# Layer 0's rounded exponential: written by ScalarE, or copied by GpSimd

## The chip, the cores and the metric

The kernel runs on one core of a Trainium2 chip. The metric is the device time of one execution in microseconds. Three runs of the kernel before took 6326.17 us in the median (6318.13 to 6328.62).

A core has engines that run side by side, each with its own queue, taken strictly in order: TensorE (PE in the profile, its weight loads PEld), VectorE (DVE), ScalarE (ACT) and GpSimd (POOL); SyncE (SP) issues the DMAs. They meet through semaphores: an instruction raises one when it is done, another engine's queue stands still until it has the value that it waits for.

## The reference

Four attention-like layers run one after the other over 32 images of 128 channels x 1024 positions. Layer 0, the one of the change, cut to what matters:

```python
xn = group_norm(x, gamma, beta)
h = xn.reshape(B, C, H * W).transpose(0, 2, 1)
q, k, v = (einsum('bnc,dc->bnd', h, W) + b for W, b in ((Wq, bq), (Wk, bk), (Wv, bv)))
attn = softmax(einsum('bnd,bmd->bnm', q, k) * C ** -0.5, axis=-1)   # 1024 x 1024, float32
out = einsum('bnm,bmd->bnd', attn, v)
out = einsum('bnd,ed->bne', out, Wp) + bp
x = out.transpose(0, 2, 1).reshape(B, C, H, W) + xn
```

Layer 1 is attention with 8 heads of 16 channels, layer 2 again full attention over 128 channels, layer 3 a linear attention.

## The kernel before, in words

**Precision.** Layers 0 and 2 multiply in the format fp32r, which keeps fewer bits than float32. To lose nothing, each operand is held as two halves: hi, the value rounded to fp32r, and lo, the difference between the exact value and hi. A product then takes three matmuls: hi x hi, hi x lo, lo x hi.

**A step of a full layer.** The 1024 x 1024 scores are handled in 16 steps of 128 keys x 512 queries, u = 0 to 15; after eight of them (T = 8) the other half of the queries begins. One step:

- TensorE, f_scores: three matmuls into p_sc.
- VectorE, f_less (L1080): fp = p_sc minus the row's maximum, in float32. fp has two buffers, u % 2.
- ScalarE, f_exp (L870, L872): fp_hi = exp(fp), rounded to fp32r as it is written; then fp = exp(fp) in place, exact. The two raise the semaphores f.p and f.pexact.
- GpSimd, f_plo (L738): waits for f.p and f.pexact and writes fp_lo = fp - fp_hi.
- GpSimd, f_add (L755, L759): adds fp to fsum, the softmax's denominator.
- TensorE, f_pv: three matmuls of fp_hi and fp_lo with the values, accumulated in p_full.

Both halves of fp_hi and fp_lo have two buffers also. f_exp of step u waits for f_pv of step u - 2, f_less of step u for the sum and fp_lo of step u - 2.

**The order of the work.** All engines play one template: a list of all pieces of work with a time each, from the table PLACE and the tables of moves (L33 to L86), sorted by that time. It mixes layer 0 of image i + 2, layer 1 of i and its neighbours, and layers 2 and 3 of i - 1, and is played once for each image. Nothing is decided at run time. So each engine's order is fixed, and an instruction that is late holds up what stands behind it in its queue, whatever layer that belongs to. In the stage of layer 0, GpSimd also has the last sum of layer 2 of another image (f_out, x3, L765) and the powers of layer 3's norms (t_norms, t_rn, L770), with which VectorE scales the keys (ka, L1158) for TensorE's t_matrix. VectorE has there the maximum of two halves for the heads (m_both, L1048). Matmuls all bear line L1224, where a helper issues them; they are told apart by their tiles: p_sc for f_scores, p_full for f_pv, p_head, p_acc and p_max for the heads of layer 1, p_chain for all the rest. ScalarE's exponentials of the heads are L903 (p <- p_head).

Below, step 12 is the step whose f_pv starts at 3226.66 us in the trace, step 13 the next.

Of the kernel before, what the change touches and what calls it, by code (L numbers as in the profile page):

```python
# [7 lines left out]
ACT = mybir.ActivationFunctionType  # L8
AX = mybir.AxisListType

C = 128
# [329 lines left out]
def heads_kernel(nc, images, x, packed, bias3, out):  # L341
    ctx = ExitStack()
    with ctx:
        def sb(name, shape, dtype=F32):
            return ctx.enter_context(nc.sbuf_tensor(name, shape, dtype))
# [50 lines left out]
        fp = [sb(f"fp{i}", [C, HALF]) for i in range(2)]  # L396
        fp_hi = [sb(f"fp{i}_hi", [C, HALF], F32R) for i in range(2)]
# [54 lines left out]
        def full(layer):  # L452
            return sem.f0 if layer == 0 else sem.f2
# [12 lines left out]
        def f32(ap):  # L466
            return ap.bitcast(F32)
# [14 lines left out]
        def after(eng, *uses):  # L482

            for signal, b, per, count in uses:
                if b.exists:
                    eng.wait_ge(signal, b.at(per, count))
                    return
# [172 lines left out]
        def _(pool):  # L660
# [72 lines left out]

            def f_plo(b, u, layer):
                f = full(layer)
                pool.wait_ge(f.p, b.at(PER.f_p, u + 1))
                pool.wait_ge(f.pexact, b.at(PER.f_pexact, u + 1))
                pool.tensor_tensor(fp_lo[u % 2][:, :], fp[u % 2][:, :], f32(fp_hi[u % 2][:, :]),  # L738
                                   ALU.subtract).then_inc(f.plo, 1)

# [27 lines left out]
            def t_norms(b):  # L768
# [4 lines left out]
            pool.wait_ge(s_folded, FOLDS)  # L773
            play(pool, dict(g_var=g_var, p_var=p_var, i_stat=i_stat, f_lo=f_lo, p_lo=p_lo,
                            f_shift=f_shift, f_vlo=f_vlo, f_plo=f_plo, f_add=f_add, f_out=f_out, t_norms=t_norms))

        @block.scalar
        def _(act):
# [79 lines left out]
            def f_exp(b, u, layer):  # L858
                f = full(layer)
                act.wait_ge(f.less, b.at(PER.f_less, u + 1))  # L860
                if u >= 2:
                    act.wait_ge(f.pv, b.at(PER.f_pv, u - 1))
                elif layer == 0:

                    after(act, (sem.f2.pv, b.shift(-3), PER.f_pv, 2 * T),
                          (sem.f0.pv, b.shift(-1), PER.f_pv, 2 * T))
                else:
                    after(act, (sem.f0.pv, b.shift(2), PER.f_pv, 2 * T),
                          (sem.f2.pv, b.shift(-1), PER.f_pv, 2 * T))
                act.activation(fp_hi[u % 2][:, :], fp[u % 2][:, :], ACT.Exp,  # L870
                               scale=float(C) ** -0.5).then_inc(f.p, 1)
                act.activation(fp[u % 2][:, :], fp[u % 2][:, :], ACT.Exp,  # L872
                               scale=float(C) ** -0.5).then_inc(f.pexact, 1)

# [50 lines left out]
            def t_leave(b, h):  # L925
# [11 lines left out]
                           bias=col("bp1")).then_inc(s_folded, 1)  # L937
            play(act, dict(g_apply=g_apply, i_apply=i_apply, p_apply=p_apply, f_hi=f_hi, p_hi=p_hi,
                           f_keep=f_keep, p_keep=p_keep, f_exp=f_exp, f_row=f_row, f_move=f_move, s_exp=s_exp,
                           s_out=s_out, t_keep=t_keep, t_turned=t_turned, t_leave=t_leave))  # L940

# [614 lines left out]
```

## Time and profile before

| what | value |
|---|---|
| median of 3 runs | 6326.17 us (6318.13 to 6328.62) |
| profiled execution, first to last instruction | 6320.3 us |
| PE busy | 5916.0 us (94%) |
| DVE busy | 4561.7 us (72%) |
| ACT busy | 4179.9 us (66%) |
| POOL busy | 3429.9 us (54%) |
| mean granted TensorE clock | 0.976 of full speed |
| chain that ended last, by engine | PE 70%, DVE 14%, ACT 7%, issue 5%, POOL 3% |

The profiled execution's own time isn't told beside its span; the span is 5.9 us below the median of the runs. A share of busy time is a mean over all stages: an engine that is busy half of the time can be full in one of them. Idle time of an engine costs something only where TensorE, or the chain that TensorE waits for, stands behind it.

### The profile page before, as it was taken

To read this page: it belongs to the slowest core of one execution; us is meant where nothing else is said; L and a number is where in the kernel's file an instruction comes from. 1 tells how busy PE (TensorE), PEld (TensorE's weight loads), DVE (VectorE), ACT (ScalarE), POOL (GpSimd) and SP (SyncE) were. 2 spreads that over 40 slices of the span, in tenths; PEclk is the share of its full clock that TensorE was granted. 3 is DMA by queue.
4 is the path that set the end of the run, shared out by engine and by line. 5 is a ranking of instruction groups with operands and counts; after the bars stand their busy time and mean duration, and the time that the engine had idled before them with its cause. 6 is when DMAs were issued, how large, how long until landed. Compare 5 with 4: busy or idle time off the path is not lost.

```text
span 6320.3 us, 81822 instructions
## 1 busy us (share of the span) xinstructions
PE 5916.0 (94%) x28562; PEld 2709.6 (43%) x28562; DVE 4561.7 (72%) x5748; ACT 4179.9 (66%) x5828; POOL 3429.9 (54%) x2739
## 2 busy tenths in 40 slices
PE   5789999999999999999999999999999999999985
PEld 2334444444444444444444444444444444444332
DVE  2677777777777777777777777777777777777742
ACT  2366776666677666777666767766677766666652
POOL 4336555556655555655555665555565555566433
PEclk7799999999999999999999999999999999999996
DMA  1011011011101101101101110110110110111000
GB/s 35 4 26 27 20 24 30 20 30 27 30 15 30 30 20 30 27 19 26 30 20 30 27 30 15 30 30 20 30 27 17 28 30 20 30 27 27 15 16 9
DMA packets 104251, 154.23 MB, mean 24 GB/s; under 512 B 64544, under 2 KB 66848, under 8 KB 103712
## 3 DMA queue, kind: packets, MB, share of 16 engines
q1 hardware_dynamic: 103840, 149.00, 10.6%
q8 instruction: 227, 3.72, 0.2%
q14 instruction: 184, 1.51, 0.1%
HBM read 18.13 MB, written 16.78 MB: 6 GB/s over the span
## 4 chain that ended last, share of the span: by engine, by line
PE 70%; DVE 14%; ACT 7%; issue 5%; POOL 3%; DMA 0%; SPq 0%; DVEq 0%; POOLq 0%; ACTq 0%
PE p_chain L1224 15%; PE p_max L1224 13%; PE p_acc L1224 11%; PE p_sc L1224 11%; PE p_full L1224 10%; PE p_head L1224 10%; DVE mx_half L1039 5%; DVE f2mx L1034 3%; POOL fp_lo L738 2%; DVE fp L1080 2%; ACT p L903 2%; ACT fp_hi L870 1%; ACT fp L872 1%; DVE f_num L1098 1%; ACT exact L847 1%
## 5 line engine op out<-in xcount | busy, mean ns | idle before, releaser
L1039 DVE TENSOR_REDUCE mx_half<-p_max 128x2 f32<-128x1024 f32 x2048 | 2507.7, 1224 | 1026.3 <-PE p_max L1224 1017.5
L903 ACT ACTIVATE p<-p_head 128x1024 f32<-128x1024 f32 x2048 | 2092.5, 1022 | 1069.8 <-PE p_head L1224 1050.6
L738 POOL TENSOR_TENSOR fp_lo<-fp,fp_hi 128x512 fp32r<-128x512 f32 x1024 | 1314.3, 1283 | 1628.4 <-ACT fp L872 1628.1
L1224 PE MATMUL p_acc<-p,v 128*17 128x512 f32 x8192 | 1086.2, 602 | 0.1
L1224 PE MATMUL p_max<-ks,qs 63*128 63x512 f32 x4096 | 975.4, 472 | 108.2 <-DVE mx_half L1039 90.7
L1224 PE MATMUL p_head<-qs,ks 64*128 64x512 f32 x4096 | 992.4, 480 | 42.5 <-ACT p L903 36.7
L759 POOL TENSOR_TENSOR fsum<-fsum,fp 128x512 f32<-128x512 f32 x768 | 991.1, 1290 | 0.0
L870 ACT ACTIVATE fp_hi<-fp 128x512 fp32r<-128x512 f32 x1024 | 640.8, 626 | 370.6 <-DVE fp L1080 311.3
L1080 DVE TENSOR_TENSOR fp<-p_sc,f_shifts 128x512 f32<-128x512 f32 x1024 | 700.7, 684 | 219.3 <-PE p_sc L1224 153.3
L1224 PEld LDWEIGHTS p_head<-qs,ks 64*128 64x128 f32 x4096 | 383.9, 184 | 932.7 <-issue 474.4
L1224 PEld LDWEIGHTS p_max<-ks,qs 63*128 63x128 f32 x4096 | 387.5, 185 | 731.0 <-DVE mx_half L1039 546.4
L872 ACT ACTIVATE fp<-fp 128x512 f32<-128x512 f32 x1024 | 634.2, 619 | 0.0
L1034 DVE TENSOR_REDUCE f0mx<-p_max 128x1 f32<-128x1024 f32 x256 | 312.8, 1222 | 139.9 <-PE p_max L1224 139.0
L1034 DVE TENSOR_REDUCE f2mx<-p_max 128x1 f32<-128x1024 f32 x256 | 312.7, 1221 | 111.5 <-PE p_max L1224 108.1
L1224 PEld LDWEIGHTS p_acc<-p,v 128*17 128x17 f32 x8192 | 135.9, 95 | 301.2 <-issue 282.8
L1224 PE MATMUL p_sc<-f0q_hi,f0k_hi 128*128 128x512 f32 x512 | 250.4, 489 | 11.7 <-DVE fp L1080 6.8
L1224 PE MATMUL p_full<-fp_hi,f0v_hi 128*128 128x512 f32 x512 | 238.2, 465 | 15.4 <-POOL fp_lo L738 15.4
L1224 PE MATMUL p_sc<-f2q_hi,f2k_hi 128*128 128x512 f32 x512 | 243.7, 476 | 7.7 <-DVE fp L1080 7.4
L1224 PE MATMUL p_full<-fp_hi,f2v_hi 128*128 128x512 f32 x512 | 233.1, 455 | 6.6 <-POOL fp_lo L738 6.6
L697 POOL TENSOR_TENSOR f2q_lo<-exact,f2q_hi 128x512 fp32r<-128x512 f32 x64 | 82.1, 1283 | 231.8 <-ACT exact L815 231.8
L1224 PE MATMUL p_sc<-f0q_hi,f0k_lo 128*128 128x512 f32 x512 | 206.1, 402 | 0.0
L1224 PE MATMUL p_sc<-f0q_lo,f0k_hi 128*128 128x512 f32 x512 | 205.3, 401 | 0.0
(187 smaller groups left out, 8118.2 us busy)
## 6 DMA issues: line engine op xcount, KB each, us to landing
qs<-cq_hi SPq DMA_DIRECT2D x128, 256.0 KB, 4.6
ks<-ck_hi SPq DMA_DIRECT2D x128, 256.0 KB, 4.2
x_in<-x_dram SPq DMA_DIRECT2D x32, 512.0 KB, 3.4
qs<-cq_lo SPq DMA_DIRECT2D x64, 256.0 KB, 4.4
ks<-ck_lo SPq DMA_DIRECT2D x64, 256.0 KB, 5.1
out_dram<-x SPq DMA_DIRECT2D x32, 512.0 KB, 2.9
o<-o SPq DMA_DIRECT2D x256, 32.0 KB, 1.9
zrow<-rz SPq DMA_DIRECT2D x128, 16.0 KB
```

The costliest lines, as they stand in the source:

```text
L697: pool.tensor_tensor(dst[1][:, half(u % 2)], exact[:, :], f32(dst[0][:, half(u % 2)]), ALU.subtract).then_inc(f.lo, 1)
L738: pool.tensor_tensor(fp_lo[u % 2][:, :], fp[u % 2][:, :], f32(fp_hi[u % 2][:, :]), ALU.subtract).then_inc(f.plo, 1)
L759: pool.tensor_tensor(dst, dst, fp[u % 2][:, :], ALU.add).then_inc(f.sum, 1)
L847: act.activation(exact[:, :], P_CHAIN[:, :], ACT.Copy).then_inc(f.vexact, 1)
L870: act.activation(fp_hi[u % 2][:, :], fp[u % 2][:, :], ACT.Exp, scale=float(C) ** -0.5).then_inc(f.p, 1)
L872: act.activation(fp[u % 2][:, :], fp[u % 2][:, :], ACT.Exp, scale=float(C) ** -0.5).then_inc(f.pexact, 1)
L903: act.activation(p1[slot][:, 2 * pr:2 * pr + 2, :], P_HEAD[:, :].rearrange("p (e n) -> p e n", e=2), ACT.Exp, scale=float(DH) ** -0.5).the ...
L1034: dve.reduce_max(f_mx[layer][:, v:v + 1], P_MAX[:, :], AX.X).then_inc(f.max, 1)
L1039: dve.reduce_max(mx_half[:, pr, :, t, kh], P_MAX[:, :].rearrange("p (e n) -> p e n", e=2), AX.X)\
L1080: dve.tensor_tensor(fp[u % 2][:, :], P_SC[:, :], f_shifts[:, :], ALU.add)\
L1098: dve.tensor_tensor(f_num[:, q], f_num[:, q], P_CHAIN[:, :], ALU.mult)\
L1224: return pe.matmul(dst, lhsT, rhs, start=start, stop=stop)
```

## The change

In layer 0 ScalarE no longer writes fp_hi. It makes only the exact exponential in place. GpSimd waits for it, copies fp to fp_hi (the copy rounds to fp32r), waits for its own copy through the semaphore f.p, and subtracts as before. In layer 2 ScalarE still writes both; there only the order of GpSimd's two waits is other.

```diff
--- before.py
+++ after.py
@@ -733,8 +733,10 @@
 
             def f_plo(b, u, layer):
                 f = full(layer)
+                pool.wait_ge(f.pexact, b.at(PER.f_pexact, u + 1))
+                if layer == 0:
+                    pool.tensor_copy(fp_hi[u % 2][:, :], fp[u % 2][:, :]).then_inc(f.p, 1)
                 pool.wait_ge(f.p, b.at(PER.f_p, u + 1))
-                pool.wait_ge(f.pexact, b.at(PER.f_pexact, u + 1))
                 pool.tensor_tensor(fp_lo[u % 2][:, :], fp[u % 2][:, :], f32(fp_hi[u % 2][:, :]),
                                    ALU.subtract).then_inc(f.plo, 1)
 
@@ -867,8 +869,9 @@
                 else:
                     after(act, (sem.f0.pv, b.shift(2), PER.f_pv, 2 * T),
                           (sem.f2.pv, b.shift(-1), PER.f_pv, 2 * T))
-                act.activation(fp_hi[u % 2][:, :], fp[u % 2][:, :], ACT.Exp,
-                               scale=float(C) ** -0.5).then_inc(f.p, 1)
+                if layer == 2:
+                    act.activation(fp_hi[u % 2][:, :], fp[u % 2][:, :], ACT.Exp,
+                                   scale=float(C) ** -0.5).then_inc(f.p, 1)
                 act.activation(fp[u % 2][:, :], fp[u % 2][:, :], ACT.Exp,
                                scale=float(C) ** -0.5).then_inc(f.pexact, 1)
```

No table of times is touched, so TensorE's and VectorE's orders stay. On GpSimd, in the middle of the program, three layer 0 steps of an image and the power of layer 3's norms stood so before (fp_lo and fsum of layer 0, t_rn of layer 3; f0_ are layer 0's semaphores):

```order
L738 TENSOR_TENSOR fp_lo<-fp,fp_hi 128x512 [waits f0_pexact,f0_p]
L759 TENSOR_TENSOR fsum<-fsum,fp 128x512 [waits f0_sum,f0_pexact]
L738 TENSOR_TENSOR fp_lo<-fp,fp_hi 128x512 [waits f0_pexact,f0_p]
L759 TENSOR_TENSOR fsum<-fsum,fp 128x512 [waits f0_sum,f0_pexact]
L738 TENSOR_TENSOR fp_lo<-fp,fp_hi 128x512 [waits f0_pexact,f0_p]
L759 TENSOR_TENSOR fsum<-fsum,fp 128x512 [waits f0_sum,f0_pexact]
L770 TENSOR_TENSOR t_rn<-t_ns,minus_half 128x16 [waits t_ns]
L738 TENSOR_TENSOR fp_lo<-fp,fp_hi 128x512 [waits f0_pexact,f0_p]
```

and the same place now:

```order
L738 CAST fp_hi<-fp 128x512 [waits f0_pexact]
L740 TENSOR_TENSOR fp_lo<-fp,fp_hi 128x512 [waits f0_p]
L761 TENSOR_TENSOR fsum<-fsum,fp 128x512 [waits f0_sum,f0_pexact]
L738 CAST fp_hi<-fp 128x512 [waits f0_pexact]
L740 TENSOR_TENSOR fp_lo<-fp,fp_hi 128x512 [waits f0_p]
L761 TENSOR_TENSOR fsum<-fsum,fp 128x512 [waits f0_sum,f0_pexact]
L738 CAST fp_hi<-fp 128x512 [waits f0_pexact]
L740 TENSOR_TENSOR fp_lo<-fp,fp_hi 128x512 [waits f0_p]
L761 TENSOR_TENSOR fsum<-fsum,fp 128x512 [waits f0_sum,f0_pexact]
L772 TENSOR_TENSOR t_rn<-t_ns,minus_half 128x16 [waits t_ns]
L738 CAST fp_hi<-fp 128x512 [waits f0_pexact]
```

Each fp_lo has a CAST, the copy, ahead of it; three more instructions stand ahead of t_rn in this piece alone, and fp_lo waits for f0_p, which the copy raises.

On ScalarE, the same steps before (fp_hi and fp of layer 0, p_0 and p_1 the heads' exponentials, o_1 a copy of the heads' output):

```order
L870 ACTIVATE fp_hi<-fp 128x512 [waits f0_pv,f0_less]
L872 ACTIVATE fp<-fp 128x512
L903 ACTIVATE p_0<-p_head 128x1024 [waits s_sc]
L911 ACTIVATE o_1<-p_acc 128x512 [waits o_pj,s_pv]
L870 ACTIVATE fp_hi<-fp 128x512 [waits f0_pv,f0_less]
L872 ACTIVATE fp<-fp 128x512
L903 ACTIVATE p_1<-p_head 128x1024 [waits s_pv,s_sc]
```

and now:

```order
L875 ACTIVATE fp<-fp 128x512 [waits f0_pv,f0_less]
L906 ACTIVATE p_0<-p_head 128x1024 [waits s_sc]
L914 ACTIVATE o_1<-p_acc 128x512 [waits o_pj,s_pv]
L875 ACTIVATE fp<-fp 128x512 [waits f0_pv,f0_less]
L906 ACTIVATE p_1<-p_head 128x1024 [waits s_pv,s_sc]
```

Between the heads' exponentials one instruction is left for each step instead of two, and it carries both waits.

## Rows read from the trace of the kernel before

**Rows 1.** Timeline of TensorE, places B and C: start us, length us, instruction, idle before
```profile
3226.66 0.50 PE L1224 MATMUL p_full<-fp_hi,f0v_hi 128*128 128x512 f32 x1 [0.31 <-POOL fp_lo L738]
...
3229.61 0.50 PE L1224 MATMUL p_full<-fp_hi,f0v_hi 128*128 128x512 f32 x1
```

**Rows 2.** Timeline of TensorE, place B one period later
```profile
3413.49 0.50 PE L1224 MATMUL p_full<-fp_hi,f0v_hi 128*128 128x512 f32 x1 [0.31 <-POOL fp_lo L738]
```

**Rows 3.** Busy time in stretches of one period: us, then each engine's, granted clock
```profile
3178.00:3200.00 22.00, 21.94 (x120) 11.72 (x119) 18.46 (x24) 14.65 (x21) 18.29 (x13) 1.00 0.00 1
...
sum 187.00, PE 181.21 PEld 83.50 DVE 142.53 ACT 130.54 POOL 107.12; mean PE 36.24 PEld 16.70 DVE 28.51 ACT 26.11 POOL 21.42
```

**Rows 4.** Waits, TensorE, whole execution: who for whom, us, times, longest
```profile
PE p_head L1224 <- ACT p L903: 36.7, 64, 1.3
...
PE p_full L1224 <- POOL fp_lo L738: 22.0, 42, 2.4
```

**Rows 5.** Waits, TensorE, layer 0 stage of one period (3164 to 3240 us)
```profile
PE p_max L1224 <- DVE mx_half L1039: 0.5, 1, 0.5
PE p_full L1224 <- POOL fp_lo L738: 0.3, 1, 0.3
```

**Rows 6.** Busy time in a stretch: the first image's layer 0 steps
```profile
54.00:106.00 52.00, 37.51 (x101) 22.69 (x101) 12.43 (x19) 19.49 (x34) 39.84 (x32) 0.76 0.00 1
```

**Rows 7.** Waits, TensorE, first image (54 to 106 us)
```profile
PE p_full L1224 <- POOL fp_lo L738: 6.0, 7, 1.3
```

**Rows 8.** Timeline of ScalarE, step 12
```profile
3224.03 0.63 ACT L870 ACTIVATE fp_hi<-fp 128x512 fp32r<-128x512 f32 x1 [1.34 <-DVE fp L1080]
3224.57 0.62 ACT L872 ACTIVATE fp<-fp 128x512 f32<-128x512 f32 x1
```

**Rows 9.** Groups of GpSimd's instructions, forms apart: count, busy us, mean ns, idle before
```profile
L738 POOL TENSOR_TENSOR fp_lo<-fp,fp_hi 128x512 fp32r<-128x512 f32 x1024 | 1314.3, 1283 | 1628.4 <-ACT fp L872 1628.1 <-POOL fsum L759 0.2
...
L765 POOL TENSOR_TENSOR x<-f_num,x 128x1024 f32<-128x1024 f32 x32 | 76.7, 2396 | 43.3 <-DVE f_num L1098 43.3
...
L720 POOL TENSOR_TENSOR f_diag<-cw,f0mx 128x512 fp32r<-128x512 f32 x64 | 66.5, 1039 | 67.9 <-PE p_sc L1224 47.9 <-DVE f0mx L1034 19.9
...
L675 POOL MEMSET qs<- 128x4096 f32 x1 | 3.6, 3566 | 0.0
...
L668 POOL MEMSET o<- 128x512 f32 x1 | 0.5, 524 | 0.0
```

**Rows 10.** Timeline of GpSimd, places B and C
```profile
3222.06 1.28 POOL L759 TENSOR_TENSOR fsum<-fsum,fp 128x512 f32<-128x512 f32 x1
3225.32 1.28 POOL L738 TENSOR_TENSOR fp_lo<-fp,fp_hi 128x512 fp32r<-128x512 f32 x1 [1.98 <-ACT fp L872]
...
3227.80 1.28 POOL L738 TENSOR_TENSOR fp_lo<-fp,fp_hi 128x512 fp32r<-128x512 f32 x1
```

**Rows 11.** Timeline of GpSimd, place A
```profile
3178.59 1.30 POOL L738 TENSOR_TENSOR fp_lo<-fp,fp_hi 128x512 fp32r<-128x512 f32 x1 [2.25 <-ACT fp L872]
...
3186.86 1.29 POOL L738 TENSOR_TENSOR fp_lo<-fp,fp_hi 128x512 fp32r<-128x512 f32 x1 [0.90 <-ACT fp L872]
...
3193.29 1.29 POOL L738 TENSOR_TENSOR fp_lo<-fp,fp_hi 128x512 fp32r<-128x512 f32 x1 [1.42 <-ACT fp L872]
...
3195.96 2.92 POOL L770 TENSOR_TENSOR t_rn<-t_ns,minus_half 128x16 f32<-128x16 f32 x1
```

**Rows 12.** Timeline of VectorE, place A
```profile
3198.92 0.29 DVE L1158 TENSOR_TENSOR ka<-tm,t_rn 128x128 f32<-128x128 f32 x1
```

**Rows 13.** Timeline of TensorE, place A
```profile
3199.69 1.94 PE L1224 MATMUL p_chain<-tm,ka 128*17 128x129 f32 x16
```

**Rows 14.** Timeline of VectorE, place B
```profile
3222.30 1.10 DVE L1048 TENSOR_TENSOR mx<-mx_half 128x32 f32<-128x32 f32 x1
```

**Rows 15.** A group of VectorE's instructions with 32-element operands
```profile
L1116 DVE TENSOR_TENSOR rz<-rz 128x32 fp32r<-128x32 f32 x64 | 12.3, 192 | 2.2
```

## The prediction, made before the change was run

> **What bounds the kernel now.** I read the stretches of one steady period first. The kernel works on several images at once and repeats itself: the matmul that starts at 3226.66 us comes again at 3413.49 us [rows 1, 2], so a period is 186.83 us and brings one image. In the 187 us cut out for the table TensorE is busy 181.21, VectorE 142.53, ScalarE 130.54 and GpSimd 107.12 [rows 3]. TensorE sets the pace, and no other engine is near it over the whole period. The average hides one stage, though: from 3178 to 3200 us, inside the layer 0 softmax, GpSimd is busy 18.29 of 22 us [rows 3]. Next I read TensorE's waits. In the whole execution it stands idle only 36.7 us for ScalarE's exponentials of the heads (64 times) and 22.0 us for fp_lo of GpSimd (42 times) [rows 4]. In the layer 0 stage of one period, 3164 to 3240 us, it has just two waits: 0.5 us for VectorE and 0.3 us for fp_lo; none for ScalarE [rows 5]. The first image is different: from 54 to 106 us TensorE is busy 37.51 of 52 us, GpSimd 39.84 [rows 6], and 6.0 us of idle time end with fp_lo [rows 7]. There the chain through GpSimd sets the time.
>
> So the change gives time to an engine that TensorE hardly waits for here (ScalarE) and takes it from one whose results TensorE does wait for at one place in each period.
>
> **The change part by part.** There are 32 images with 16 layer 0 steps, so 512 steps. Each loses one ScalarE instruction: the next one started 0.54 us after it (3224.03 to 3224.57) [rows 8]. The exact exponential is thus ready 0.54 us sooner. In its place GpSimd gets a copy of 128x512 numbers and, since fp_lo now waits for GpSimd's own copy, a handoff. Layer 2's waits merely change places, and both were met by the time the second one was: nothing.
>
> *The copy, c.* No GpSimd copy stands in the trace. From below: the memset of 128x512 takes 524 ns [rows 9]. From above: the two-input subtraction of the same size takes 1283 ns, and the one whose inputs are broadcast 1039 ns [rows 9]. The memsets of 512 and 4096 elements (524 and 3566 ns) give 0.849 ns an element. The two-input form of 512 and 1024 elements (1283 and 2396 ns) gives 2.17 ns an element and 0.17 us fixed [rows 9]. A copy reads once and writes once; I take the memset's pace and the fixed part of an instruction that reads: 0.849 x 512 + 0.17 = 0.61 us, an estimate. It lies nearest the memset row.
>
> *The handoff, h.* From ScalarE's end (3224.57 + 0.62 = 3225.19) to fp_lo's start at 3225.32 is 0.13 us [rows 8, 10]; its bounds are 0 and that. I take 0.12. So a step adds c + h = 0.73 us of GpSimd, between 0.52 and 1.41. Behind the waiting fp_lo stand, in GpSimd's queue, the running sum (VectorE may not refill that fp buffer before it) and once an image x3 and t_rn; TensorE's p_full waits for fp_lo itself.
>
> *Place A, 3178 to 3200 us.* GpSimd goes from the fp_lo at 3178.59 to the end of t_rn's power, 3195.96 + 2.92 = 3198.88, with just 0.90 and 1.42 us of idle time [rows 11]. Five layer 0 steps lie in it: 5 x 0.73 = 3.65 us more. The start comes 0.54 sooner and the idle 2.32 is used up: t_rn ends 3.65 - 0.54 - 2.32 = 0.79 us later. Behind it VectorE scales the keys (3198.92 + 0.29 = 3199.21) [rows 12], and TensorE uses them at 3199.69 [rows 13]. Of those 0.48 us about 0.05 is TensorE's own handoff (fp_lo's end 3226.60 to its user's start 3226.66 [rows 1, 10]), so 0.43 is slack and 0.36 us becomes a wait.
>
> *Place B, step 12.* Before, fp_lo ran 3225.32 to 3226.60 and TensorE started at 3226.66 after waiting 0.31 us [rows 1, 10]: no slack. The copy alone makes it 0.73 - 0.54 = 0.19 later. But there is a second effect. VectorE's 32-element maximum of two SBUF operands began at 3222.30 and took 1.10 us, ending with the GpSimd sum that had begun at 3222.06 (until 3223.34) [rows 10, 14]; another operation of VectorE with 128x32 operands in SBUF takes 192 ns [rows 15]. So VectorE was held by the GpSimd instruction in flight, and step 12's shift comes behind it. After the change GpSimd runs later there: two copies in front less 0.54 put the sum at 3222.06 + 1.46 - 0.54 = 3222.98, so an fp_lo is in flight at 3222.30 and ends near 3223.03. VectorE is let go about 0.34 sooner. B = 0.19 - 0.34 = -0.15. If it isn't let in between the two instructions it goes with the sum's end, 0.92 later than before: B is between -0.15 and +1.1. I take -0.15.
>
> The Trainium skill (SBUF — State Buffer, "Who interferes with whom") says that a VectorE instruction with two SBUF inputs contends with a GpSimd instruction that reads SBUF, and that whichever issues first holds the other for its whole length. The trace agrees at this one place: 1.10 us against 0.192.
>
> *Place C, step 13.* Its fp_lo ended at 3227.80 + 1.28 = 3229.08 and was used at 3229.61 [rows 1, 10]: 0.48 us of slack beyond the handoff. GpSimd goes from step 12's fp_lo through a sum to it without a gap, so now it ends B + 0.73 = 0.58 later, and TensorE starts it 0.10 later than before. B and C together cost 0.10 us.
>
> *Sum.* A + B + C = 0.46 us a period; the waits at either place don't overlap. (6320.3 less some 700 us of filling and draining) / 186.83 is 30 periods: 14 us. The first image has no cover: 16 x 0.73 = 11.7 us more GpSimd work against 12.2 us of idle time in its 52 us [rows 6], most of it at the two starts of a half, where it can't be used; I let half of the work through, 6 us, and 1 us for the second image. Together 21 us on the profiled execution's 6320.3 us span. The runs' median, 6326.17, is 5.9 us above that span, so 6326 + 21 = 6347 us.
>
> *At the ends.* With c + h = 0.52 place A has slack left, and B and C win about 0.3 us a period (the hold ends sooner and step 13 stays covered): -9 + 4 = -5, so 6321. With the broadcast row, c + h = 1.16: A is 5.80 - 2.86 - 0.43 = 2.51, B 0.62, C another 0.62 + 1.16 - 0.62 - 0.48 = 0.68; 3.8 x 30 + 12 = 126, so 6452. With the two-input row, 1.41: A 3.76, B 0.87, C 0.93; 5.6 x 30 + 16 = 184, so 6510.
>
> **The rivals.** *The copy runs at a two-input pace (1.0 us or more).* For it: every GpSimd instruction in the trace that reads two 128x512 operands takes 1.04 to 1.28 us. Against it: a copy reads one operand. Time 6452 to 6510; chance 0.17. *The copy lies between, 0.75 to 0.9 us.* Half way between the forecast's 0.61 and 1.04 the terms give some 70 us: 6396; chance 0.2.
>
> The Trainium skill (GPSIMD Engine Reference, "Elementwise — side-by-side cycle accounting") gives 769 ns for 512 elements in the best loop and "RD/WR-port-bound at 1.03 cyc/elem" for simple bodies; with the first the sum would be about 67 us, 6393, with the second near my estimate. No row here shows which a copy follows.
>
> *ScalarE's relief wins (the other side).* Mechanism: 8.6 us less ScalarE queue a period (16 x 0.54) brings the heads' exponentials forward, and TensorE's p_head matmuls with them. All that it can give as waits is 36.7 / 30 = 1.2 us a period [rows 4], and in the layer 0 stage there is none [rows 5], so it would have to come as matmuls that start a little sooner; I give it a third to a half of the 1.2, 0.4 to 0.7 us. It decides when c + h is under about 0.6, so that A, B and C cost nothing: 30 x 0.4 to 0.7 = 12 to 21 us, 6305 to 6314. Chance 0.1. *ScalarE was off the path and GpSimd's slack takes it all*: 6326, chance 0.08. The forecast has 0.45.
>
> **How the numbers follow.** A measurement of this kernel can tell 0.2% (12.7 us) from no change. Faster takes most of the relief case: 0.08. Same takes the neutral case, the rest of the relief case and a quarter to a third of the forecast's own spread (c + h below 0.69): 0.26. Slower takes the rest, 0.66. The range of 8 in 10 goes from 6312 to 6455: it takes in the low end and the broadcast row, and leaves out the two-input price and the best of the relief.
>
> **What would show it.** ScalarE busy falls by 512 x 0.62, about 320 us; GpSimd's rises by 512 x c, 312 us at my price: that row decides most. Place A: a wait of TensorE for the keys (ka) of 0.3 to 0.4 us in each period, and GpSimd without a gap from step 2 to t_rn. Place B: the wait for fp_lo at step 12 about 0.15 shorter than 0.31, VectorE's maximum at about 0.75 instead of 1.10 us. Place C: a new wait for fp_lo of about 0.25 us at step 13. The period grows from 186.83 to 187.3 us. Wrong: a copy over 0.75 us, a period below 186.8, or new waits in stages where layer 0's GpSimd work isn't.

## The result: 0.3 per cent slower

| | before | after |
|---|---|---|
| median of the compared runs, us | 6324.93 | 6345.24 (6341.49 to 6348.88) |
| ratio, with its 95% interval | | 1.0032 (1.002 to 1.0043) |
| profiled execution, span / run time, us | 6320.3 | 6343.7 / 6345.46 |

The change costs 20 us (13 to 27). The page of the changed kernel shows the moved work. These are its engines' line, the head of the chain and two groups (count, busy us, mean ns, idle before):

```profile
PE 5922.4 (93%) x28562; PEld 2709.2 (43%) x28562; DVE 4574.8 (72%) x5748; ACT 3932.4 (62%) x5316; POOL 3739.5 (59%) x3251
...
PE 64%; POOL 13%; DVE 13%; ACT 4%; issue 4%; DMA 0%; SPq 0%; POOLq 0%; DVEq 0%; ACTq 0%
...
L740 POOL TENSOR_TENSOR fp_lo<-fp,fp_hi 128x512 fp32r<-128x512 f32 x1024 | 1318.9, 1288 | 630.1 <-ACT fp L875 589.1
...
L738 POOL CAST fp_hi<-fp 128x512 fp32r<-128x512 f32 x512 | 312.6, 610 | 702.3 <-ACT fp L875 702.1
```

A copy takes 610 ns, 512 of them 312.6 us. Of ScalarE's busy time 247 us are gone, and not the 320 forecast: neighbours overlap there (0.54 us from start to start, 0.62 long), so a removed instruction takes less busy time with it than its length: the lengths alone fell by 314 us. GpSimd's share of the chain that ended last rose from 3 to 13 per cent. TensorE's waits in the whole execution (us, times, longest) answer to [rows 4]:

```profile
PE p_head L1227 <- ACT p L906: 36.5, 63, 1.3
PE p_full L1227 <- POOL fp_lo L740: 24.8, 53, 2.3
PE p_chain L1227 <- DVE ka L1161: 17.9, 30, 4.9
```

Busy time in stretches of one period, with place A in the first, answers to [rows 3]:

```profile
3192.00:3215.00 23.00, 22.39 (x126) 12.02 (x125) 19.31 (x24) 12.29 (x15) 22.52 (x19) 1.00 0.00 1
...
sum 187.00, PE 180.69 PEld 83.13 DVE 142.68 ACT 122.56 POOL 116.45; mean PE 36.14 PEld 16.63 DVE 28.54 ACT 24.51 POOL 23.29
```

GpSimd is busy 22.52 of 23 us there. Of TensorE's waits, the one for ScalarE is what it was (36.7). The one for fp_lo has 53 places instead of 42. That for the keys (ka) is new; before, it came once.

**Where in the period.** TensorE's first score matmul of an image is the mark of a period. Before, the marks of images 0, 1, 4, 17 and 31:

```profile
54.82 0.77 PE L1224 MATMUL p_sc<-f0q_hi,f0k_hi 128*128 128x512 f32 x1 [1.58 <-DVE f_shifts L1060]
...
194.71 0.79 PE L1224 MATMUL p_sc<-f0q_hi,f0k_hi 128*128 128x512 f32 x1
...
735.40 0.40 PE L1224 MATMUL p_sc<-f0q_hi,f0k_hi 128*128 128x512 f32 x1
...
3164.31 0.40 PE L1224 MATMUL p_sc<-f0q_hi,f0k_hi 128*128 128x512 f32 x1
...
5780.52 0.40 PE L1224 MATMUL p_sc<-f0q_hi,f0k_hi 128*128 128x512 f32 x1
```

After, the same marks, and behind the fourth the places A, B and C of that period:

```profile
56.17 0.77 PE L1227 MATMUL p_sc<-f0q_hi,f0k_hi 128*128 128x512 f32 x1 [1.58 <-DVE f_shifts L1063]
...
203.07 0.80 PE L1227 MATMUL p_sc<-f0q_hi,f0k_hi 128*128 128x512 f32 x1
...
745.64 0.40 PE L1227 MATMUL p_sc<-f0q_hi,f0k_hi 128*128 128x512 f32 x1
...
3178.23 0.40 PE L1227 MATMUL p_sc<-f0q_hi,f0k_hi 128*128 128x512 f32 x1
...
3214.04 1.92 PE L1227 MATMUL p_chain<-tm,ka 128*17 128x129 f32 x16 [0.45 <-DVE ka L1161]
...
3240.82 0.50 PE L1227 MATMUL p_full<-fp_hi,f0v_hi 128*128 128x512 f32 x1 [0.30 <-POOL fp_lo L740]
...
3243.98 0.51 PE L1227 MATMUL p_full<-fp_hi,f0v_hi 128*128 128x512 f32 x1 [0.15 <-POOL fp_lo L740]
...
5797.80 0.40 PE L1227 MATMUL p_sc<-f0q_hi,f0k_hi 128*128 128x512 f32 x1
```

Between images 4 and 31 lie 27 periods: 5045.12 us before, 5052.16 after, so 186.86 and 187.12 us each, +0.26. The first period grew from 139.9 to 146.9 us, images 1 to 4 together by 1.9 more. The first mark is 1.4 us later, the part behind the last one 6.1 longer. The five add up to the spans' 23.4 us. The first mark isn't the change's work, since no copy has run by then: the kernel before with another VectorE instruction (4 below) has it at 56.27.

Inside the period I give the distance from the mark to three matmuls, as medians over some 25 periods: the use of the keys (A), step 12's p_full (B), step 13's p_full (C). The period is the mean of 27, and each row comes from one trace.

| kernel | A | B | C | period | first |
|---|---|---|---|---|---|
| before | 35.41 | 62.37 | 65.32 | 186.86 | 139.9 |
| after | 35.82 | 62.59 | 65.75 | 187.12 | 146.9 |
| one-input maximum, before | 35.38 | 62.07 | 65.00 | 186.55 | 139.9 |
| one-input maximum, after | 35.84 | 62.62 | 65.78 | 187.13 | 146.2 |
| no copy in step 7 | 35.43 | 62.19 | 65.34 | 186.72 | 146.5 |
| waits exchanged alone | 35.41 | 62.23 | 65.18 | 186.57 | 138.9 |
| copies in four steps | 35.30 | 61.93 | 64.87 | 186.26 | 139.4 |

GpSimd of the changed kernel, places A and B to C (timeline):

```profile
3206.90 0.61 POOL L738 CAST fp_hi<-fp 128x512 fp32r<-128x512 f32 x1
3207.59 1.28 POOL L740 TENSOR_TENSOR fp_lo<-fp,fp_hi 128x512 fp32r<-128x512 f32 x1
3208.83 1.47 POOL L761 TENSOR_TENSOR fsum<-fsum,fp 128x512 f32<-128x512 f32 x1
3210.26 2.91 POOL L772 TENSOR_TENSOR t_rn<-t_ns,minus_half 128x16 f32<-128x16 f32 x1
3213.14 0.61 POOL L738 CAST fp_hi<-fp 128x512 fp32r<-128x512 f32 x1
...
3237.14 1.29 POOL L761 TENSOR_TENSOR fsum<-fsum,fp 128x512 f32<-128x512 f32 x1
3238.74 0.61 POOL L738 CAST fp_hi<-fp 128x512 fp32r<-128x512 f32 x1 [0.32 <-ACT fp L875]
3239.43 1.32 POOL L740 TENSOR_TENSOR fp_lo<-fp,fp_hi 128x512 fp32r<-128x512 f32 x1
```

and VectorE at the same places:

```profile
3213.21 0.68 DVE L1161 TENSOR_TENSOR ka<-tm,t_rn 128x128 f32<-128x128 f32 x1 [0.43 <-POOL t_rn L772]
...
3236.60 0.63 DVE L1051 TENSOR_TENSOR mx<-mx_half 128x32 f32<-128x32 f32 x1
...
3238.90 0.49 DVE L1117 CAST rz<-rz 128x32 fp32r<-128x32 f32 x1
```

and ScalarE's exponential of step 12:

```profile
3238.05 0.63 ACT L875 ACTIVATE fp<-fp 128x512 f32<-128x512 f32 x1 [1.07 <-DVE fp L1083]
```

From copy to fp_lo are 0.69 us (3238.74 to 3239.43): 0.61 and a handoff of 0.08. The copy itself starts 0.06 us behind ScalarE's end (3238.68), where fp_lo started 0.13 behind it before. So the change adds 0.69 us to a step in which GpSimd is busy anyway, and 0.62 to one in which it waits for ScalarE. The maximum takes 0.63 us instead of the 1.10 of [rows 14]. New is the other VectorE row: the scaling of the keys takes 0.68 instead of the 0.29 of [rows 12]. It starts at 3213.21, while the copy of step 7 runs (3213.14 to 3213.75), and ends behind it. The copy has one input, and still holds VectorE's operation with two. The copy of step 12 lies over a VectorE cast of 32 columns, which takes 0.49 us where it took 0.18 before; no new wait of TensorE follows there.

### The profile page after: what moved, and what is told of

It reads as the page before. It is cut to its first block, busy times and chain, and to the rows that moved or that the text cites. A ratio compares the mean times of both kernels' runs of the same rounds, so it can differ in the third digit from the quotient of the medians.

```text
span 6343.7 us, 81310 instructions
## 1 busy us (share of the span) xinstructions
PE 5922.4 (93%) x28562; PEld 2709.2 (43%) x28562; DVE 4574.8 (72%) x5748; ACT 3932.4 (62%) x5316; POOL 3739.5 (59%) x3251
## 4 chain that ended last, share of the span: by engine, by line
PE 64%; POOL 13%; DVE 13%; ACT 4%; issue 4%; DMA 0%; SPq 0%; POOLq 0%; DVEq 0%; ACTq 0%
PE p_chain L1227 15%; PE p_max L1227 12%; PE p_acc L1227 10%; PE p_sc L1227 10%; PE p_full L1227 9%; PE p_head L1227 8%; POOL fp_lo L740 5%; DVE mx_half L1042 4%; POOL fsum L761 4%; DVE f2mx L1037 3%; POOL fp_hi L738 2%; DVE fp L1083 2%; POOL t_rn L772 1%; POOL x L767 1%; ACT fp L875 1%
## 5 line engine op out<-in xcount | busy, mean ns | idle before, releaser
L1227 PE MATMUL p_head<-qs,ks 64*128 64x512 f32 x4096 | 990.3, 479 | 40.5 <-ACT p L906 36.5
L738 POOL CAST fp_hi<-fp 128x512 fp32r<-128x512 f32 x512 | 312.6, 610 | 702.3 <-ACT fp L875 702.1
L873 ACT ACTIVATE fp_hi<-fp 128x512 fp32r<-128x512 f32 x512 | 320.2, 625 | 82.8 <-DVE fp L1083 75.5
```

The source lines that it names most:

```text
L738: pool.tensor_copy(fp_hi[u % 2][:, :], fp[u % 2][:, :]).then_inc(f.p, 1)
L1227: return pe.matmul(dst, lhsT, rhs, start=start, stop=stop)
```

## The experiments

Each ran beside the kernel before on its own chip; differences below are between those medians. Three sets of four ran on three chips, so ratios are compared across sets, not times.

**1. No copies at all.** In layer 0 neither ScalarE nor GpSimd writes fp_hi, and GpSimd waits for the exact exponential alone. At the start of the program GpSimd clears the two fp_hi buffers once (here and in 9).

```diff
-                act.activation(fp_hi[u % 2][:, :], fp[u % 2][:, :], ACT.Exp, ...).then_inc(f.p, 1)
+                if layer == 2:
+                    act.activation(fp_hi[u % 2][:, :], fp[u % 2][:, :], ACT.Exp, ...).then_inc(f.p, 1)
```

> Layer 0 without any rounding into fp_hi: ScalarE writes only the exact exponential, GpSimd copies nothing, and fp_lo and TensorE read what stands in fp_hi from layer 2 (left out: layer 0's rounded half). Theory (fixed queues, three tight places): TensorE gets back the 0.31 us a period that the trace of the changed kernel shows at the heads' scores, and the wait of about 0.3 us at step 12 goes; 28 x 0.6 = 17 us and some 2 us of the first image, so 6306 us against 6325. Rival (ScalarE is off the path, its time is worth nothing): 6325 us. Second rival (what costs is the longer chain of each step): as the first number or a little less.

Measured: 6331.24 us against 6321.81, ratio 1.0017 (1.0008 to 1.0026). The theory missed, and with it its rival: less work on two engines made the kernel slower. The first image won 3.7 us (136.2), but the period is 187.24. VectorE's timeline at step 12:

```profile
3227.70 1.18 DVE L1120 CAST rz<-rz 128x32 fp32r<-128x32 f32 x1
3228.91 1.23 DVE L1122 TENSOR_TENSOR rz<-rz 128x32 fp32r<-128x32 f32 x1
3230.06 0.68 DVE L1086 TENSOR_TENSOR fp<-p_sc,f_shifts 128x512 f32<-128x512 f32 x1
```

GpSimd's at the same time, an fp_lo and a sum that lie over the first two:

```profile
3227.56 1.28 POOL L743 TENSOR_TENSOR fp_lo<-fp,fp_hi 128x512 fp32r<-128x512 f32 x1 [1.71 <-ACT fp L878]
3228.80 1.29 POOL L764 TENSOR_TENSOR fsum<-fsum,fp 128x512 f32<-128x512 f32 x1
```

TensorE's, the wait that follows:

```profile
3230.79 0.50 PE L1230 MATMUL p_sc<-f0q_hi,f0k_hi 128*128 128x512 f32 x1 [0.36 <-DVE fp L1086]
```

The cast of 32 columns takes 1.18 us, and the subtraction behind it 1.23; free, the same subtraction takes 0.192 on average [rows 15]. Because ScalarE was earlier, GpSimd's step 12 slid from behind this pair to over it. VectorE's next fp comes late, and TensorE waits behind it. That was a new theory; experiment 9 tests it.

**2. The copy without ScalarE's relief.** ScalarE keeps a second exponential for each layer 0 step, written where nobody reads it.

```diff
+                else:
+                    act.activation(fp_lo[u % 2][:, :], fp[u % 2][:, :], ACT.Exp, ...)
```

> The changed kernel with ScalarE's second exponential put back: it writes it, rounded, to fp_lo's buffer, which the subtraction overwrites, so the result is the same. Theory: without the 0.54 us that ScalarE gave back, place A costs 5 x 0.68 - 2.32 - 0.43 = 0.65 us and the hold by the copy 0.4, step 12 about 0.8, step 13 about 0.2, and the 0.31 us at the heads' scores are gone: 2.0 x 28 + 9 = 65 us over before, 6390 us. Rival (ScalarE's relief is worth nothing in the changed kernel): 6345 us.

Measured: 6397.18 us against 6321.81, ratio 1.0119 (1.0105 to 1.0134); period 188.80. TensorE waits for fp_lo 49.8 us in 65 places. The theory holds in the main, with 75 us over before where 65 were expected. Its split of place A doesn't: the scaling of the keys isn't held here (0.29 us), and t_rn ends 1.6 us later than before instead of 1.1. Inside the change the relief is worth 0.87 per cent, some 55 us, because each exponential is ready 0.54 us sooner and GpSimd needs that time.

**3. Two copies in each step.** GpSimd makes the copy twice.

```diff
+                    pool.tensor_copy(fp_lo[u % 2][:, :], fp[u % 2][:, :])
                     pool.tensor_copy(fp_hi[u % 2][:, :], fp[u % 2][:, :]).then_inc(f.p, 1)
```

> The changed kernel with a second GpSimd copy of the same size in front of each first one (into fp_lo's buffer): c + h goes from 0.68 to 1.29 us. Theory: place A 5 x 1.29 - 0.6 - 2.32 - 0.43 = 3.1 us and 0.3 of hold, B 0.7, C 0.6, less the 0.31 that ScalarE gives: 4.4 x 28 + 14 = 137 us over before, 6462 us; that is 5.7 times the 20 us of the first copy, since the slack is used up. Rival (cost in proportion to the copy: 20 us for each): 6365 us. Second rival (the chain of each step decides, 0.57 us at step 12 and 13 only): 28 x 1.1 + 27 = about 6385 us.

Measured: 6525.33 us against 6321.81, ratio 1.032 (1.0307 to 1.0334); period 192.99. The direction is the theory's, the size isn't: 204 us instead of some 140. TensorE's waits:

```profile
PE p_full L1228 <- POOL fp_lo L741: 104.8, 119, 2.7
...
PE p_chain L1228 <- DVE ka L1162: 39.8, 30, 4.9
...
PE p_chain L1228 <- POOL x L768: 23.2, 31, 3.3
```

The first two are the places I had. The third, layer 2's last sum (x3) behind the copies, was no term of mine. So the price of GpSimd time isn't constant: it climbs as slack ends at more places.

**4. The maximum with one input.** In the kernel before, VectorE's maximum of two halves becomes two reductions, each with one SBUF input.

```diff
-                dve.tensor_tensor(mx1[...], two[:, :, :, :, 0], two[:, :, :, :, 1], ALU.max)
+                dve.reduce_max(out[:, 0], two[:, 0], AX.X)
+                dve.reduce_max(out[:, 1], two[:, 1], AX.X)
```

> The kernel before, with VectorE's maximum of two SBUF operands (m_both) made as two reductions over pairs, each with one SBUF input; same values. Theory (the GpSimd instruction in flight holds VectorE there): it no longer lasts 1.10 us, step 12's subtraction starts some 0.3 us sooner and the wait of 0.31 us for fp_lo goes: 28 x 0.3 = 8 us less, 6317 us. Rival (the 1.10 us are VectorE's own, or something else holds step 12): 6325 us.

Measured: 6313.49 us against 6321.81, ratio 0.9988 (0.9979 to 0.9997); period 186.55. The group row (count, busy us, mean ns, idle before):

```profile
L1049 DVE TENSOR_REDUCE mx<-mx_half 128x16 f32<-128x32 f32 x64 | 11.6, 181 | 1.1
```

Each of the two takes under 0.19 us where the maximum took 1.10, though a GpSimd instruction is in flight at 122 of the 128, and B comes 0.30 us sooner. The hold at place B was real and cost the kernel before about 8 us (2 to 13).

**5. All copies but step 7's.** In the changed kernel, step 7 of each image is done the old way (here and in 6 to 8 and 12 the copies raise a semaphore of their own, and f.p counts the other steps; the diffs show the condition alone). The copy that lay over ka is gone; nothing ahead of t_rn is.

```diff
-                if layer == 0:
+                if layer == 0 and u != 7:
                     pool.tensor_copy(fp_hi[u % 2][:, :], fp[u % 2][:, :])
```

> The changed kernel, except that in step 7 of each image ScalarE still writes fp_hi and GpSimd makes no copy. Step 7's copy is the one that lay over VectorE's scaling of the keys (ka), which took 0.68 us instead of 0.29, and it stood ahead of fp_lo and of the power t_rn's followers. Theory (the GpSimd copy itself holds VectorE's two-input operation, and that is the part of place A that the prediction missed): ka is back at 0.29 us or the wait behind ka loses 0.3 to 0.4 us a period, the period is about 186.7 instead of 187.06 us, and the time about 10 us under the changed kernel's, some 10 us over the kernel before (6332 where before is 6322). Rival (place A is only the later end of t_rn, which step 7 does not move): no change against the changed kernel, 20 us over the kernel before.

Measured: 6330.63 us against 6323.48, ratio 1.0013 (1.0004 to 1.0022), where the changed kernel's is 1.0032; period 186.72. VectorE's timeline:

```profile
2831.93 0.29 DVE L1174 TENSOR_TENSOR ka<-tm,t_rn 128x128 f32<-128x128 f32 x1 [0.43 <-POOL t_rn L785]
```

The theory holds, nearly to the number. t_rn ends 34.95 us after the mark (2831.90 less 2796.95), as in the changed kernel (34.94), but ka takes 0.29 again, and A is at 35.43, 0.02 behind the kernel before. So t_rn's later end by itself costs TensorE next to nothing, and the one copy of step 7 costs 0.40 us a period by what it holds (187.12 less 186.72). The edit also puts ScalarE's second exponential back in that step, but ka is shorter by 0.39 us, as much as the period. That is most of the steady loss: the period is now under the kernel before's, and 0.15 us over that of experiment 10, which has the new order of the waits and no copy.

**6. The first image the old way.** Image 0's steps without copies, all others with them (the same condition, on the image).

> The changed kernel, except that image 0's 16 steps are done the old way (ScalarE writes both, no copy). Theory (the first image has no other work to cover GpSimd, and gives 7.0 us of the whole): the first image's period is 139.9 us again instead of 146.9, the time 7 us under the changed kernel's, some 13 us over before. Rival (the first image's delay is taken back by slack later): the same as the changed kernel, 20 us over before.

Measured: 6334.44 us against 6323.48, ratio 1.0019 (1.001 to 1.0028). The first period is 138.8 us, the others stay at 187.09. That is 1.1 us under the kernel before, and what the exchange of the waits gives there by itself (138.9 in 10); so the copies cost the first image 8.1 us, of which the exchange returns 1.1. Against the changed kernel this is 0.13 per cent, some 8 us, with intervals that overlap. The marks say it more sharply: from the first to the last they lie 5732.9 us apart instead of 5741.6. What the first image loses reaches the end and isn't taken back.

**7. Copies in four steps.** Steps 2, 3, 10 and 11 the new way, the other twelve the old.

```diff
-                if layer == 0:
+                if layer == 0 and u in (2, 3, 10, 11):
                     pool.tensor_copy(fp_hi[u % 2][:, :], fp[u % 2][:, :])
```

> Layer 0's steps 2, 3, 10 and 11 alone get the new way (ScalarE writes only the exact exponential, GpSimd copies); the other twelve stay. Theory (what the change costs sits in steps 4 to 9 and 12 to 15, where GpSimd has no idle time or TensorE waits for fp_lo; what it gains comes from ScalarE's relief where GpSimd has idle time): none of the new waits, and up to 0.3 to 0.6 us less a period: 10 to 16 us under before. Rival (ScalarE's relief is worth nothing by itself, as the run without copies suggests, and any earlier ScalarE is taken back by a VectorE operation that GpSimd then holds): within 5 us of before or a little slower.

Measured: 6306.56 us against 6323.48, ratio 0.9977 (0.9967 to 0.9986); period 186.26. Faster than before and after, as the theory has it. But these steps bring the new order of the waits with them, which the theory hadn't priced: experiment 10's period is 186.57, so ScalarE's relief gives 0.31 us of the 0.60. The wait for fp_lo fell from 22.0 us in 42 places to 13.2 in 13:

```profile
PE p_full L1240 <- POOL fp_lo L753: 13.2, 13, 2.3
```

**8. Four steps and the one-input maximum.**

> The same four steps, and VectorE's maximum of two halves made as two reductions with one SBUF input each, so that GpSimd does not hold it. Theory (the hold and the relief are separate and add): the gain of the four steps plus the 8 us that the one-input maximum gave by itself, 15 to 24 us under before. Rival (both shorten the same wait at step 12, so they do not add): no better than the one-input maximum alone, about 8 us under before.

Measured: 6303.87 us against 6323.48, ratio 0.9974 (0.9965 to 0.9984); period 186.27. The time alone decides nothing: 19.6 us under before lies in the theory's range, and the rival's 8 us didn't come. The periods decide: those of 7 and 8 are the same, so the two don't add, as the rival has it. In 7 the maximum at step 12 takes 0.64 us instead of 1.10 as it is.

**9. No copies, ScalarE's second exponential back in step 12.** The test of what experiment 1 suggested.

```diff
-                if layer == 2:
+                if layer == 2 or u == 12:
                     act.activation(fp_hi[u % 2][:, :], fp[u % 2][:, :], ACT.Exp, ...)
```

> The run without copies once more (layer 0's fp_hi is not computed, ScalarE makes one exponential a step), except that in step 12 ScalarE again makes its second one, so that GpSimd's fp_lo starts 0.54 us later there, behind VectorE's cast and subtraction of 32 columns for the heads' denominators and not over them. Theory (those two took 1.18 and 1.23 us instead of 0.18 and 0.19 because GpSimd held them, and that alone made the run without copies slower than before): both are back at 0.2 us, the new waits of TensorE behind them (1.5 us a period) go for 0.3 us at step 12, the period falls from 187.2 to about 186.0 us, and the time is 22 to 30 us under before. Rival (the run without copies was slow for another reason, so that giving work back to ScalarE can only cost): 10 us over before, or more.

Measured: 6292.09 us against 6324.23, ratio 0.995 (0.9936 to 0.9963); period 185.96. One ScalarE instruction *more* for each image makes the kernel some 40 us faster than in experiment 1. VectorE's pair there:

```profile
2835.15 0.18 DVE L1122 CAST rz<-rz 128x32 fp32r<-128x32 f32 x1
2835.37 0.19 DVE L1124 TENSOR_TENSOR rz<-rz 128x32 fp32r<-128x32 f32 x1
```

and GpSimd's fp_lo of step 12:

```profile
2835.53 1.29 POOL L743 TENSOR_TENSOR fp_lo<-fp,fp_hi 128x512 fp32r<-128x512 f32 x1 [2.21 <-ACT fp L880]
```

fp_lo starts when the pair is nearly done, and both are short. The theory's numbers (186.0 us, 22 to 30 us under before) were met and a little passed. It also says what ScalarE's relief is worth where it does no harm: 0.5 per cent less the 0.14 that the exchanged waits give by themselves (10; these two kernels have them too), some 23 us. Experiment 1's loss came from 1.0 us of held VectorE, twice, in one place. Experiment 1's period is 1.28 us longer than this kernel's, and over the whole execution TensorE waits 35 us longer for VectorE: for the maxima of the heads 106.0 us instead of 90.7, for fp 27.2 instead of 15.3, for o 11.2 instead of 3.0.

**10. The two waits exchanged alone.** The kernel before, GpSimd waiting for pexact first and then for p, in both layers.

```diff
-                pool.wait_ge(f.p, b.at(PER.f_p, u + 1))
                 pool.wait_ge(f.pexact, b.at(PER.f_pexact, u + 1))
+                pool.wait_ge(f.p, b.at(PER.f_p, u + 1))
```

> The kernel before, with only the order of GpSimd's two waits ahead of fp_lo exchanged, as the change did it (pexact first, then f.p), in both layers. Theory (the wait that ends last must be the one that the instruction's queue meets first: in the changed kernel's trace layer 2's fp_lo starts 0.077 us after ScalarE's end where it was 0.141 before, though the prediction put that part at nothing): every fp_lo that waits for ScalarE starts 0.065 us sooner, TensorE's wait at step 12 is 0.25 us instead of 0.31, the period 0.06 us shorter, 2 us in all, so 0 to 4 us under before. Rival (the 0.065 us come from something else, ScalarE's fewer instructions or the other traffic): the gap stays at 0.14 us and the time as before.

Measured: 6315.64 us against 6324.23, ratio 0.9986 (0.9977 to 0.9994); period 186.57. ScalarE's timeline at step 12:

```profile
2844.55 0.62 ACT L872 ACTIVATE fp<-fp 128x512 f32<-128x512 f32 x1
```

GpSimd's fp_lo behind it:

```profile
2845.24 1.28 POOL L738 TENSOR_TENSOR fp_lo<-fp,fp_hi 128x512 fp32r<-128x512 f32 x1 [1.91 <-ACT fp L872]
```

and TensorE's use of it:

```profile
2846.58 0.50 PE L1224 MATMUL p_full<-fp_hi,f0v_hi 128*128 128x512 f32 x1 [0.25 <-POOL fp_lo L738]
```

From the exponential's end (2845.17) to fp_lo are 0.07 us; before it was 0.13 [rows 8, 10]. Over all steps with nothing else in front, the median fell from 0.142 to 0.077 us. The theory holds and was too small: it had 0 to 4 us, and 8.6 came (4 to 15). The wait at step 12 is 0.25 us, as it said, but the period fell by 0.29 us instead of 0.06. Of these 0.14 are there by place C and the rest comes behind it, where layer 2's steps lie. The table bears this out: from C to the next mark are 121.35 to 121.39 us in every row with the new order, and 121.54 and 121.55 in the two rows without it.

**11. The changed kernel with the one-input maximum** (the edit of 4).

> The changed kernel, with VectorE's maximum of two halves as two reductions with one SBUF input each, which GpSimd does not hold. Theory (the change had already shortened this hold from 1.10 to 0.63 us, the prediction's term of -0.34 us at step 12, and step 13 is bound by GpSimd's own chain from there): the maximum has nothing more to give, the period stays at 187.06 us, and the time is 17 to 22 us over before, while the same edit of the kernel before won 8 us. Rival (the two are separate): the period falls by 0.3 us as it did in the kernel before, and the time is 8 us less than the changed kernel's, 12 us over before.

Measured: 6344.26 us against 6324.23, ratio 1.0031 (1.002 to 1.0041); period 187.13. The same edit gave 8 us before and nothing that can be told after (1.0031 against 1.0032). The change had used up what it could give, which is the evidence for term B's negative sign.

**12. Copies in eight steps,** 0 to 3 and 8 to 11.

> Layer 0's steps 0 to 3 and 8 to 11 get the new way, eight of sixteen. Theory (the gain of the four steps 2, 3, 10 and 11 is capped by TensorE's wait for VectorE's tm ahead of step 4 and by step 12's fp_lo, so that more steps with slack add nothing): within 4 us of the four steps' time, 13 to 21 us under before. Rival (ScalarE's relief adds up with the number of steps as long as GpSimd has idle time): twice the gain, 30 us under before.

Measured: 6304.79 us against 6324.23, ratio 0.9967 (0.9954 to 0.9979); period 186.22 against 186.26 with four. The theory holds: the other four copies give nothing that can be told.

Experiments 7, 8 and 12 beat both kernels and can't be told from each other. About half of their gain is the exchange of the waits, which came with them (10 alone: 0.14 per cent; 7: 0.23). The other half is real: on one chip all five runs of 12 (up to 6305.51 us) lie under all eleven of 10 (from 6307.11).

## Why the prediction was right, and where it wasn't

It said 6347 us; the runs gave 6345.24. The likeliest case was the one that came, but the agreement is closer than its terms deserve, and in part luck: of the forecast 14 us of steady loss 7 came, and in the profiled executions about as much came at the start and the end, where nothing was forecast.

- **The copy, c.** 0.61 estimated, 610 ns measured. The memset's pace and one fixed part was the row to go by; both dearer rivals fall with it.
- **The handoff, h.** 0.12 was too much. Half of the 0.13 that I read was the order of two waits. GpSimd to itself it is 0.08, so c + h is 0.69, not 0.73. Where GpSimd waits for ScalarE, as at step 12, it is 0.62, since the copy also starts sooner than fp_lo did.
- **Layer 2's waits, "nothing".** Wrong: a term was put at nothing without a test. The wait for p is met half a us ahead of the one for pexact, so their order seemed free, but fp_lo started 0.065 us sooner behind the later one in the new order. Alone that is worth 0.14 per cent, 8.7 us (10). Against that kernel, which has the new order already, the change costs 0.55 us a period.
- **Place A.** Forecast 0.36, measured 0.41 (35.41 to 35.82), by another mechanism. t_rn ends only 0.4 us later (34.94 after the mark instead of 34.57; forecast 0.79, of which 5 x 0.04 is the handoff's error), which TensorE's slack covers. The cost is step 7's copy over ka (5). I had used the very same hold as a gain at place B and hadn't looked for it at the other places where GpSimd's work moves.
- **Place B.** Forecast -0.15, measured -0.19 (+0.22 at B less the +0.41 brought along). The maximum took 0.63 us; I had said about 0.75. The term of 0.34 was right: step 12's fp starts 1.01 us behind its first score matmul (3237.29 less 3236.28) instead of 1.34 (3223.32 less 3221.98). (My own end for fp_lo, 3223.03, would have given 0.31.) The sign that I named was wrong, though: the wait at B did not shrink but stayed at 0.30 us, since TensorE came there sooner too: its weight load for the next scores waits 0.20 us for VectorE's fp instead of 0.35. Experiments 4 and 11 confirm the mechanism.
- **Place C.** B and C together 0.10 forecast, 0.02 measured (+0.43 at C); the new wait is there, 0.15 us instead of 0.25. At C the whole shift is 0.43 us, where the sum said 0.46.
- **Behind C** nothing was forecast; 0.17 us come back there, with layer 2's steps, where the exchanged waits work: every kernel with them has it, with or without copies (10). So the period grew by 0.26 and not by 0.46: 7 us instead of 14.
- **First image.** Forecast 6 and 1 us; measured 7.0 and, for the next three together, 1.9. Experiment 6 shows that it counts in full. One stretch (us, busy of PE, PEld, DVE, ACT, POOL, granted clock) answers to [rows 6]. GpSimd is busy 44.28 us instead of 39.84, and the granted clock is 0.70 instead of 0.76; no run tells how much of the 7.0 us is the clock's:

```profile
56.00:108.00 52.00, 36.70 (x91) 22.09 (x91) 11.10 (x18) 9.99 (x16) 44.28 (x44) 0.70 0.00 1
```

- **ScalarE's relief as a rival.** I priced it by TensorE's waits for the heads, 0.4 to 0.7 us a period. Those didn't move (36.5 us). The relief came through GpSimd's earlier start: 55 us inside the change (2), some 23 by itself (9). The list of TensorE's waits for ScalarE didn't show it.

7.0 + 7.0 + 1.9 make 16 of the 20 us. In the profiled executions the rest is in the start (1.4) and behind the last mark (6.1). Of the 6.1 us the last image's own layer 0 steps account for 0.5; the others come later. The last stretch before (us, busy of PE, PEld, DVE, ACT, POOL, granted clock):

```profile
5780.00:6320.00 540.00, 429.81 (x1954) 189.37 (x1953) 273.02 (x357) 277.31 (x376) 209.03 (x161) 0.89 0.07 15
```

and after:

```profile
5797.00:6343.00 546.00, 437.23 (x1956) 191.00 (x1954) 273.73 (x357) 269.92 (x361) 218.98 (x177) 0.87 0.07 15
```

TensorE isn't idle for longer (108.8 us against 110.2); it is busy for 7.4 us more with as many matmuls, at a lower clock. The same 80 us of the last images show it best, before:

```profile
5980.00:6060.00 80.00, 66.81 (x337) 25.99 (x338) 52.99 (x65) 41.96 (x50) 12.30 (x10) 0.91 0.14 31
```

and after:

```profile
5997.00:6077.00 80.00, 68.68 (x312) 26.56 (x310) 49.79 (x62) 39.50 (x47) 10.65 (x8) 0.80 0.13 31
```

TensorE ran more of it at 1.2 GHz (0.80 against 0.91 on average). Over all kernels here this last part is 537 to 548 us long. Experiments 2 and 3 have it longest (547.7 and 546.6), and the others have no order that I could tie to their edits: 536.7 without step 7's copy, 543.0 with the one-input maximum on top of the change. Whether the last 4 us belong to the change stays open.

## What to carry to other kernels

A moved instruction is priced by more than its length: list every short instruction of the other engine that it could hold, here VectorE's with two SBUF inputs and its casts, and see over which of them it comes to lie after the move; one collision in a period can outweigh all the queue time. Where two waits stand ahead of an instruction, look at which of them is met last, and try both orders; it cost nothing here and was worth 0.14 per cent. And an edit that shows no gain everywhere may show one in the steps where the receiving engine has idle time: four steps of sixteen won 0.23 per cent, 0.14 of it by the exchanged waits, where all sixteen lost 0.32.

## What the runs showed of the hardware that I had not expected

- GpSimd's one-input copy holds VectorE's two-input operation as its two-input instructions do: ka 0.68 us instead of 0.29.
- VectorE's cast of 128x32 from and to SBUF, with one input, was held too: 1.18 us against 0.18 (1 and 9), and 0.49 under the changed kernel's copy. The Trainium skill (SBUF — State Buffer, "Who interferes with whom") counts casts that run in a two-port mode among those that contend, and says that reductions on this chip don't. The traces agree in so far as a cast was held, though no row tells in which mode it ran, and the reductions of experiment 11 took 0.18 to 0.19 us with a GpSimd subtraction in flight.
- The order of two waits ahead of one GpSimd instruction: 0.142 us from ScalarE's end to the start with the wait that is met last written last, 0.077 us with it written first. No run tells which part of the engine the 0.065 us are spent in.
- Less work can be slower by a collision alone: 1.0017 without any copy (1), 0.995 with one more exponential an image (9).
